# Reading the next tile's expert number behind the up-products, on TensorE's sequencer

## The reference, cut to what matters

```python
xn = _layernorm(x)
# layer 0: 16 experts, hidden width 128, each token goes to 4 of them
g = silu(einsum('th,efh->tef', xn, w1_e))
u = einsum('th,efh->tef', xn, w3_e)
routed = einsum('tef,ehf,te->th', g * u, w2_e, combine)
# layer 1: 8 experts, hidden width 512, each token goes to 2 of them
h1 = einsum('bsd,efd->bsef', xn, W1)
h2 = einsum('bsd,efd->bsef', xn, W2)
expert_out = einsum('bsef,edf->bsed', silu(h1) * h2, W3)
```

## Time and profile before

| | us |
|---|---|
| median of 3 runs | 2373.49 (2372.2 to 2376.42) |
| profiled execution | 2380.25 |
| its span, first to last instruction | 2378.5 |

### The profile page before, as it was taken

How to read it: one execution, slowest core, us unless ns; L and a number is a source line. 1 busy time by engine, 2 the same in 40 slices (tenths; PEclk the granted TensorE clock), 3 DMA queues, 4 the chain that set the end, 5 groups by cost and what they waited for, 6 DMA issues and landing times. The chain is left out here.

```text
span 2378.5 us, 40732 instructions
## 1 busy us (share of the span) xinstructions
PE 2186.9 (92%) x12292; PEld 1587.3 (67%) x12292; DVE 1596.0 (67%) x3508; ACT 1187.8 (50%) x2671; POOL 1425.0 (60%) x1272
## 2 busy tenths in 40 slices
PE   4879999999999999999999989998688779999997
PEld 2446777777777777777777767776344656666665
DVE  4778888888888888888888745665777732222222
ACT  2456777777777777777777622222132331111111
POOL 1326777777777777777777756776634114444443
PEclk9989999999999999999999999999789899999999
DMA  9854445554454544445455368663630055222221
GB/s 325 312 131 129 143 142 148 147 151 143 134 145 145 160 140 141 138 146 152 143 151 138 103 190 269 215 190 120 237 115 1 1 183 161 46 47 43 44 44 20
DMA packets 193827, 329.02 MB, mean 138 GB/s; under 512 B 49235, under 2 KB 135508, under 8 KB 193364
## 3 DMA queue, kind: packets, MB, share of 16 engines
q1 hardware_dynamic: 137220, 232.12, 32.6%
q0 software_dynamic: 26880, 53.64, 8.8%
q10 hardware_dynamic: 29520, 40.66, 5.3%
HBM read 240.46 MB, written 86.79 MB: 138 GB/s over the span
## 5 line engine op out<-in xcount | busy, mean ns | idle before, releaser
L1014 DVE SCALAR_TENSOR_TENSOR m_cv<-m_hp,conv,m_cv 128x256 f32<-128x256 f32 x864 | 416.5, 482 | 112.2 <-ACT m_cv L913 91.0
L1405 PE MATMUL e_u<-wup,e_xgT 128*128 x1152 | 421.1, 498 | 8.3 <-issue 4.2
L1343 ACT ACTIVATE e_sil<-e_u 128x128 f32<-128x128 f32 (+1 forms) x216 | 83.0, 384 | 551.8 <-PE e_u L1405 519.9
L840 POOL TENSOR_TENSOR m_er<-m_er,m_cT 128x1024 f32<-128x1024 f32 x128 | 302.1, 2360 | 45.5 <-DVE m_ar L1021 45.5
L951 ACT ACTIVATE m_ar<-m_ar,m_ta 128x128 f32<-128x128 f32 x1024 | 318.9, 391 | 0.8
L1102 PE MATMUL m_hp<-xnT,wpj 128*128 128x259 f32 x1152 | 305.5, 388 | 7.5 <-PEq L145 4.5
L1405 PEld LDWEIGHTS e_u<-wup,e_xgT 128*128 128x128 f32 x1152 | 203.2, 191 | 140.0 <-issue 128.6
L1110 PE MATMUL m_gp<-xnT,wpj 128*128 128x256 f32 x1024 | 268.8, 384 | 11.2 <-ACT m_gT L931 11.2
L1102 PEld LDWEIGHTS m_hp<-xnT,wpj 128*128 128x128 f32 x1152 | 214.9, 193 | 68.8 <-issue 29.1
L1300 POOL DMA_INDIRECT out<-e_y,target x72 | 113.0, 1570 | 228.9 <-DVE e_y L1374 202.3
L847 POOL TENSOR_TENSOR m_hdd<-m_hdt,m_tb 128x512 f32<-128x512 f32 x128 | 131.0, 1043 | 193.5 <-DVE m_hdt L1029 193.5
(11 more groups left out here) (313 smaller groups left out, 3951.6 us busy)
## 6 DMA issues: line engine op xcount, KB each, us to landing
m_ar<-acum_rows_dram SPq DMA_DIRECT2D x512, 128.0 KB, 3.7
m_er<-eacum_rows_dram SPq DMA_DIRECT2D x128, 512.0 KB
rows_by_slot<-blank_rows ACTq DMA_DIRECT2D x1, 18576.0 KB, 81.7
e_xg<-rows_by_slot ACTq DMA_DIRECT2D x132, 129.0 KB
m_xrow<-xn_rows SPq DMA_DIRECT2D x32, 512.0 KB
b_work<-y_rows SPq DMA_DIRECT2D x16, 1024.0 KB, 7.0
wup<-in_w SPq DMA_DIRECT2D x8, 1024.0 KB
wpj<-in_w_proj SPq DMA_DIRECT2D x1, 4352.0 KB, 23.7
```

The source lines that it names most:

```text
L840: g.tensor_tensor(er[:, t], er[:, t], middle(cT[:, t * P:(t + 1) * P], HQ), ALU.mult).then_inc(scaled.sem, 1)
L1014: v_.scalar_tensor_tensor(o, hp[n % 2][:, j:j + BLK], conv[:, c, j:j + 1], o, ALU.mult, ALU.add).then_inc(tapped.sem, 1)
L1405: ins = nc.tensor.matmul(u_ps[a.slot(2)][b][:, 0:width], xgT[:, a.slot(2), c, :], wup[:, c, ds(e * (2 * f) + b * width, width)], start=c = ...
```

## The change

One call is added to TensorE's loop, behind the up-products of tile n-1 and ahead of the transposes of tile n-2's hidden values: the expert number of tile n is read there. As `expert` keeps what it has read, the call ahead of tile n's up-products, in the next step, then finds the register and issues nothing. In step 0, where there are no up-products, the number of tile 0 is read behind its x-transposes.

```diff
@@ -1406,6 +1406,8 @@
                                                        wup[:, c, ds(e * (2 * f) + b * width, width)],
                                                        start=c == 0, stop=c == KD - 1)
                         ins.then_inc(s_up, 1)
+                    if s.inside(nt):
+                        expert(s)
                     b = s.back(2)
                     if b.inside(nt):
                         reached(pe, s_hk, b, 1)
```

## The result

The changed kernel takes 2349.33 us (median of four runs, 2347.89 to 2354.6), the kernel before 2372.87 in four runs beside it (2372.2 to 2376.42). The ratio is 0.9898, with an interval of 0.9886 to 0.991: faster by about 24 us, where 17.7 were forecast (2356). Its profiled execution took 2354.6, with a span of 2352.9; it is the slowest of the four, 5.3 above their median.

The account below looks back on a forecast made before the run. The first stage was taken as bound by TensorE's sequencer, its load held behind the x_ps copy. Savings of 13.9, 3.5 and 0.3, together 17.7 us, took the median 2373.49 to 2356; forecast's own range 2350 to 2364, wider range 2345 to 2368.

Parts of the forecast that it names:

- The stage and the wait: First expert stage only: the number's load, held behind the x_ps copy, idles TensorE 23.8 us before up-products; this wait goes.
- 0.1 a step: First stage, ahead of the h-transposes: about 0.1 us of idle array per step moves there.
- The rival of a renamed wait: The hid wait releases the sequencer instead of the copy, or the move fails otherwise: no gain, 2373; chance 0.09.
- The rival in which the load isn't held: Sequencer passes the x-transposes' wait, so the load is done before the copy; moving it gives nothing, 2373; chance 0.02.
- 1.70 a step: First stage after the change: the sequencer's own loop bounds undisturbed steps at 1.70 us, down from 1.81.
- the full floor: Rival: loads shorten to 0.30, the array's 1.63 a step bounds the first stage; 27.6 us saved, 2346; chance 0.14.
- 13.9 for 126 steps: First stage: 126 undisturbed steps each save 0.11 us, together 13.9 us.
- Seven pairs, 3.5 us: First stage, every 11 tiles beside the join's DMAs: seven slow pairs of steps save 0.5 us each, 3.5 together.
- The start of the second stage, 0.3 us: Second expert stage: its first load gets out from behind a copy, saving 0.3 us, between 0 and 0.7.
- A longer stall beside the join's DMAs: First stage: sign that the prediction is wrong, if the saved time came back as such a stall; no size given.
- Slower: Rival: load length counts in every step from a mean load of 0.46; at 0.696, 28 us lost, 2401; chance 0.09.

Follow-up runs that it names:

- the third set: Set of runs in which the unchanged kernel before was profiled once more: 2374.46 us, ratio 1.0001.
- the second: Set of runs in which the changed kernel was run once more, without further change: 2351.61 us, ratio 0.9894 to the kernel before.
- variant with two buffers: The changed kernel with two x_ps buffers in turn, so x-transposes wait for the copy of the tile before the last: 2349.27 us, ratio 0.9901.

## Why the prediction was right, and where it was off

**The stage and the wait: right.** Nothing happened in the second stage (5.82 a step, as forecast), everything in the first. Loads begin with U (0.08 ahead of it in the median) and no longer behind a copy, the wait ahead of the up-products is gone, and the sequencer passes the hid wait without stopping: 0.7 us of idle time ahead of the h-transposes in the whole stage. The prediction had put 0.1 a step there, some 14 us in all; that didn't come, as the step is the array's 1.63 and holds hardly any idle time. The rival of a renamed wait is out by the same rows. It would have been right had the call been placed one group later: the load behind the h-transposes met the hid wait and got under half of the gain. The new place is the only one of the four tried that is ahead of both waits. The rival in which the load isn't held is out too: the new order would have changed nothing by it.

**The term that was mis-sized: 1.70 a step.** The next bound was named rightly, the sequencer's own loop against the array's 1.63, but sized with the loads of the old place: 1.30 of other work, 0.35 for the mean load, 0.03 behind the check, and 0.02 more because slow ones count in full. Measured are 1.644. The mean load is 0.313 in its new place, its maximum 0.533 instead of 0.696; from start to start of its operations, with the medians of all, the sequencer's loop adds up to 1.617, just below the array's 1.63. So the array binds in most steps, and the rest puts 0.014 on the mean step, not 0.07. That the loads would stay as they were, "and this doesn't change", was the reason given against the full floor, and it fell: the DMA share of the stage is higher after (0.74 against 0.67 in the earlier trace rows), and the loads are shorter all the same. The likeliest case in hindsight was the full floor of 1.63, whose 22.7 for the plain steps (0.18 each) is close to what follows; the time of its case, 2346, is 3 below the measured one, 2356 is 7 above it.

**The sum, made again.** The two profiles without disturbed pairs are that of before in the third set and that of the changed kernel in the second. 140 steps went from 1.822 to 1.646, 24.6 us. The new stall takes back 4.0, half of it by the clock behind it, and 20.6 remain, against 20.7 from line 1394 (261.9 to 241.2) and 20.5 in the spans (2372.2 to 2351.7). The prediction had 13.9 for 126 steps. By medians the kernel gains 23.5 and 23.1 in its two sets. The two profiled executions used here lie 0.5 below and 1.8 above the medians of their kernels, 2.3 together, which makes 22.9 of the 20.6; what moves single executions by that much isn't known, and this is as far as the sum can be closed.

**Seven pairs, 3.5 us: near in size by chance.** They were taken for a property of the kernel. They are there on some chips and not on others, and the median of the kernel before (2372.87 beside the changed one) lies with the 2374 of the chips without them. The profiled execution was 6.8 above its median, and the pairs are worth 269 - 261.9 = 7.1 us, by which the stage is longer in the first of its two profiles, with 6.3 in the spans. That the 6.8 are these same 7 us is a reading: the changed kernel's first profiled execution is 5.3 above its median without any pair. By the reading the saving had to be counted with 140 plain steps, not 126 and seven pairs, and the 14 further steps give 2.5 at 0.18 each, not 3.5. The prediction carried the 6.8 over to the changed kernel as they were; there they were 5.3.

**The start of the second stage, 0.3 us: not to be told.** Its second step took 5.63 and 5.82 in two profiles of the kernel before, 6.23 and 5.50 in two of the changed one: the scatter is larger than the term.

**A longer stall beside the join's DMAs** was named as what would make the prediction wrong, with no price. It came in this way: the join's work on GpSimd is tied to tile numbers, the arrival of its rows to time. It took 4.0 of 24.6 us, and half of them by a fall of the granted clock behind the wait, of which the prediction has nothing. The prediction asked GpSimd only for its load a step (1.6), and not what it waits for when the tiles come earlier.

**Slower.** The price of the rival held: what is beyond the array's floor counts in about full, 0.73 for a second load with its check (0.66 by durations, and 0.08 by the first loads, which grew). Its condition, a mean load over 0.46, was far from met.

## What to carry to other kernels

A load of a number into a register, with its bound check, held TensorE's sequencer for 0.65 us here, and it didn't start before the waits ahead of it were met. So look for a place behind a long group that is queued for the array, and ahead of every wait of the step; to free it of one wait of two was worth between a fifth and under a half of the gain. Where an engine works off its operations in order, as VectorE did with the hidden multiply and the copy, two waits can be one. When a stage gets faster, look for work that is tied to its step numbers but fed by transfers tied to time: here one constant, raised from 54 to 58, took that stall away. A short stall of the array cost twice its length here, as the granted clock fell behind it. And before a pattern in one profile goes into a sum, take a second profile, on another chip if there is one: on the chip with long steps beside the join about half of the gain was left.

## What was not expected of the hardware

The same load of four bytes has another length at each place of the step: 0.31 us on the mean behind the up-products and behind the h-transposes, 0.35 behind the wait for the copy, 0.40 behind the down-product, 0.41 behind x-transposes that don't wait; the least is 0.295 or 0.296 in each of the five. What lengthens it is open. The "Latency and other measured facts" of DMA: Bandwidth & Descriptors in the Trainium skill, with some 600 ns as the floor, again doesn't fit: 144 loads have a median of 302 ns.

The kernel before takes 2374 us on two chips and 2382 on two others. Two kernels were profiled on a chip of each kind. The changed one with FIRST = 58 differs by 11.2 us in its spans and by 13.4 in the stage, in steps beside the join's groups, in which ScalarE's silu begins late, 0.6 and 1.3 us in the two shown. The one with the load behind the h-transposes differs by 14.2 in the spans and by only 7.9 in the stage; the rest lies outside of it, and its cause is open.

A wait of 1.9 to 2.1 us of the array, in the middle of a stage that kept it busy, was followed by the lower clock level in two profiles of the changed kernel, and one of 1.8 in its variant with two buffers wasn't.
